# A router stage with its steps pipelined one batch deeper

## The reference

```
h = h + gated @ Wproj + bproj              # gated: the gated heads, (tokens, 256)
x = layernorm(h)                           # over the 256 columns of a token
logits = x @ router_w.T + experts_bias     # (tokens, 8)
rw, sel = top_k(logits, 2); rw = softmax(rw)
moe = sum over the 2 chosen experts of rw * (silu(x w1) * (x w3)) w2,  plus a shared expert
```

## Time and profile before

| | us |
|---|---|
| median of 3 runs | 1509.64 |
| profiled execution, first to last instruction | 1589.0 |
| block `out_route` in it, about | 845 to 955 |
| PE, DVE, ACT busy in 843 to 957 | 71.1, 58.0, 41.8 of 114 |
| granted TensorE clock in 843 to 957 | 0.75 |

### The profile page before, as it was taken

One profiled execution on the slowest core, in us unless ns is written; L12 is line 12 of the kernel. 1 busy time (PEld: TensorE's weight loads), 2 busy tenths in 40 slices (PEclk: granted clock), 3 DMA queues, 4 the chain that ended last, 5 costly groups with the idle time before them and its releaser, 6 DMA issues. The chain is left out here.

```text
span 1589.0 us, 29472 instructions
## 1 busy us (share of the span) xinstructions
PE 1285.5 (81%) x9695; PEld 992.9 (62%) x9696; DVE 852.7 (54%) x1794; ACT 662.1 (42%) x1260; POOL 664.7 (42%) x616
## 2 busy tenths in 40 slices
PE   6878999999978769918996767129986999989997
PEld 3655555555557657706664547119985888878886
DVE  4996677676738849965553554104432333333332
ACT  3872556555655544403453332003332333333332
POOL 7856566665341206772000001760002454544553
PEclk9995799888989977858997778558997999999999
DMA  1678889888300036643533110000017534365331
GB/s 50 195 254 247 231 241 250 232 233 212 89 1 1 1 106 185 184 130 88 119 68 115 44 40 8 8 1 27 33 34 267 129 53 125 59 196 130 54 53 21
DMA packets 122865, 179.26 MB, mean 113 GB/s; under 512 B 26052, under 2 KB 83820, under 8 KB 122772
## 3 DMA queue, kind: packets, MB, share of 16 engines
q1 hardware_dynamic: 105876, 159.62, 34.5%
q0 software_dynamic: 16896, 18.44, 6.9%
HBM read 104.73 MB, written 74.31 MB: 113 GB/s over the span
## 5 line engine op out<-in xcount | busy, mean ns | idle before, releaser
L1629 DVE TENSOR_REDUCE att_top<-att_psS 128x4 f32<-128x512 f32 (+2 forms) x192 | 195.2, 1039 | 79.4 <-PE att_psS L1516 78.8
L2773 POOL DMA_INDIRECT out<-ffn1c_y,ffn1c_table x72 | 113.3, 1574 | 179.4 <-ACT ffn1c_y L2886 91.0
L2762 POOL DMA_INDIRECT ffn1c_rows<-normed_rows,ffn1c_table x72 | 71.0, 987 | 151.1 <-DVE ffn1c_gate L2934 127.4
L2914 DVE TENSOR_TENSOR ffn1c_hid<-ffn1c_psG,ffn1c_sil 128x512 f32<-128x512 f32 x72 | 49.8, 692 | 144.9 <-PE ffn1c_psG L2814 144.9
L1600 ACT ACTIVATE att_prob<-att_psS 128x1024 f32<-128x1024 f32 (+1 forms) x96 | 83.7, 886 | 78.7 <-PE att_psS L1530 78.6
L1510 PE MATMUL att_psS<-pairs_ka,pairs_qa 48*128 48x384 f32 (+3 forms) x512 | 107.4, 428 | 8.3 <-DMA pairs_ka<-k_parts 4.1
L2814 PE MATMUL ffn1c_psG<-ffn1c_w_h,ffn1c_xh 128*128 x288 | 97.5, 420 | 11.5 <-DMA ffn1c_w_l<-experts_lo 4.7
L1600 ACT ACTIVATE pairs_part<-att_psS 128x1024 f32<-128x1024 f32 (+1 forms) x96 | 83.3, 887 | 52.1 <-PE att_psS L1530 52.1
L1530 PE MATMUL att_psS<-pairs_qa,pairs_ka 50*128 50x256 f32 (+3 forms) x512 | 95.7, 418 | 3.3 <-DVE att_top L1629 1.1
L2650 DVE TENSOR_TENSOR ffn1b_act_f<-ffn1b_psG,ffn1b_sil 128x256 f32<-128x256 f32 x64 | 27.2, 425 | 126.4 <-remote 63.3
L2814 PE MATMUL ffn1c_psG<-ffn1c_w_l,ffn1c_xh 128*128 x288 | 91.0, 397 | 0.0
(11 more groups left out here) (397 smaller groups left out, 3577.4 us busy)
## 6 DMA issues: line engine op xcount, KB each, us to landing
prep_raw<-in_w_all SPq DMA_DIRECT2D x27, 512.0 KB, 6.9
experts_hi<-ffn0w_room SPq DMA_DIRECT2D x27, 512.0 KB, 3.9
experts_lo<-prep_lo SPq DMA_DIRECT2D x27, 512.0 KB, 4.7
ffn1c_w_h<-experts_hi SPq DMA_DIRECT2D x8, 1536.0 KB, 6.5
ffn1c_w_l<-experts_lo SPq DMA_DIRECT2D x8, 1536.0 KB, 10.9
qkv_near<-near_keys SPq DMA_DIRECT2D x32, 320.0 KB, 4.3
q_parts<-pairs_part SPq DMA_DIRECT2D x8, 1024.0 KB
k_parts<-pairs_part SPq DMA_DIRECT2D x16, 512.0 KB
```

The lines of the kernel that those rows point to most:

```text
L1629: dve.tensor_reduce(dst, src, AX.X, ALU.max).then_inc(s["max"], 1)
L2762: pool.indirect_dma_start(out=rows[:, t.buf, :], out_offset=None, in_=dram["rows"], in_offset=bass.IndirectOffsetOnAxis(ap=table[:, t.valu ...
L2773: pool.indirect_dma_start(out=rows_out, in_=y[:, t.buf, :], in_offset=None, out_offset=bass.IndirectOffsetOnAxis(ap=table[:, t.value:t.val ...
L2914: dve.tensor_tensor(hid[:, t.par, :], psG[:, t.par, 1, :], sil[:, t.par, :], ALU.mult).then_inc(s["act"], 1)
```

## The change

The steps are reordered and one more is added (B+3). In step n, PE now projects batch n, turns the logits of n-3, turns rows of n-1, turns attention of n+2 and makes logits of n-2. Two batches of attention are turned and split on PE and ACT before the loop. ACT's list becomes: copy the sums of n-3, split rows of n-1, split attention of n+2, root of n, normed n. DVE adds each half of the projection and at once takes its statistics, then aggregates; it splits rows before it adds the bias; bias and pick are of n-3. The turned sums get a bank of their own, `psL`, with the waits that go with it. DVE's wait for the bias load comes after the first `low_attention`.

```diff
--- before.py
+++ after.py
@@ -116,8 +116,14 @@
             k.sem(f"{name}_{n}") for n in "stats mv dev root rstd shift".split())
 
     def dve_gather(self, dve, res, b):
-        for t in range(TG * b, TG * (b + 1)):
+        self.dve_stats(dve, res, range(TG * b, TG * (b + 1)))
+        self.dve_aggregate(dve, b)
+
+    def dve_stats(self, dve, res, tiles):
+        for t in tiles:
             dve.bn_stats(self.stats[:, t, :], res[:, t, :]).then_inc(self.s_stats, 1)
+
+    def dve_aggregate(self, dve, b):
         for t in range(TG * b, TG * (b + 1)):
             dve.wait_ge(self.s_stats, t + 1)
             dve.bn_aggr(self.mv[:, t, :], self.stats[:, t, :]).then_inc(self.s_mv, 1)
@@ -2135,7 +2141,7 @@
         none = k.sb("none", [P, D])
         empty = k.sb("empty", [P, TILES, 2], I32)
         psA, psX = k.ps("psA", [P, KD, S]), k.ps("psX", [P, KD, S])
-        psY, psR = k.ps("psY", [P, 2, 512]), k.ps("psR", [P, 512])
+        psY, psR, psL = k.ps("psY", [P, 2, 512]), k.ps("psR", [P, 512]), k.ps("psL", [P, 512])
         s = {n: k.sem(n) for n in ("bias hi wt names logT0 none empty filler blank aT ah al y res xn xT xh xl logT_ps logT "
                                    "log_ps log best place placef gap exp hot share").split()}
         s_raw = [k.sem(f"raw{n}") for n in range(len(ws))]
@@ -2214,7 +2220,7 @@
             def logits(b):
                 pe.wait_ge(s["xl"], KD * (b + 1))
                 if b >= 1:
-                    pe.wait_ge(s["log"], b)
+                    pe.wait_ge(s["logT"], b)
                 n = 0
                 for m, x in split_passes(w_r["hi"], w_r["lo"], xh, xl):
                     for c in range(KD):
@@ -2224,23 +2230,26 @@
 
             def turn_logits(b):
                 pe.wait_ge(s["logT"], b + 1)
+                if b >= 1:
+                    pe.wait_ge(s["log"], b)
                 for i in range(TG):
-                    mm = pe.transpose(psR[:, P * i:P * (i + 1)], logT[:, P * i:P * (i + 1)], ident[:])
+                    mm = pe.transpose(psL[:, P * i:P * (i + 1)], logT[:, P * i:P * (i + 1)], ident[:])
                 mm.then_inc(s["log_ps"], 1)
 
             turn_attention(0)
+            turn_attention(1)
             pe.wait_ge(s["wt"], len(ws))
-            for n in range(B + 2):
+            for n in range(B + 3):
+                if n < B:
+                    project(n)
+                if 0 <= n - 3 < B:
+                    turn_logits(n - 3)
+                if 0 <= n - 1 < B:
+                    turn_rows(n - 1)
+                if n + 2 < B:
+                    turn_attention(n + 2)
                 if 0 <= n - 2 < B:
                     logits(n - 2)
-                if n + 1 < B:
-                    turn_attention(n + 1)
-                if n < B:
-                    project(n)
-                if 0 <= n - 2 < B:
-                    turn_logits(n - 2)
-                if 0 <= n - 1 < B:
-                    turn_rows(n - 1)
 
         @block.scalar
         def _(act):
@@ -2268,19 +2277,21 @@
             def logits(b):
                 act.wait_ge(s["logT0"], 1)
                 act.wait_ge(s["logT_ps"], b + 1)
+                if b >= 1:
+                    act.wait_ge(s["log_ps"], b)
                 act.copy(logT[0:E1N, :], psR[0:E1N, :]).then_inc(s["logT"], 1)
 
             high_attention(0)
-            for n in range(B + 2):
-                if 0 <= n - 2 < B:
-                    logits(n - 2)
-                if n + 1 < B:
-                    high_attention(n + 1)
+            high_attention(1)
+            for n in range(B + 3):
+                if 0 <= n - 3 < B:
+                    logits(n - 3)
+                if 0 <= n - 1 < B:
+                    high_rows(n - 1)
+                if n + 2 < B:
+                    high_attention(n + 2)
                 if n < B:
                     own.act_root(act, tiles_of(n), n)
-                if 0 <= n - 1 < B:
-                    high_rows(n - 1)
-                if n < B:
                     normed(n)
             act.wait_ge(s["gap"], 1)
             act.activation(gap[:], gap[:], ACT.Exp).then_inc(s["exp"], 1)
@@ -2295,11 +2306,10 @@
                     dve.tensor_tensor(al[:, b % 2, c, :], psA[:, c, :], ah[:, b % 2, c, :].bitcast(F32), ALU.subtract
                                       ).then_inc(s["al"], 1)
 
-            def add(b):
-                for q in range(2):
-                    dve.wait_ge(s["y"], 2 * b + q + 1)
-                    r = res[:, TG * b + 2 * q:TG * b + 2 * q + 2, :]
-                    dve.tensor_tensor(r, r, psY[:, q, :].rearrange("p (t d) -> p t d", d=D), ALU.add).then_inc(s["res"], 1)
+            def add(b, q):
+                dve.wait_ge(s["y"], 2 * b + q + 1)
+                r = res[:, TG * b + 2 * q:TG * b + 2 * q + 2, :]
+                dve.tensor_tensor(r, r, psY[:, q, :].rearrange("p (t d) -> p t d", d=D), ALU.add).then_inc(s["res"], 1)
 
             def low_rows(b):
                 for c in range(KD):
@@ -2309,7 +2319,7 @@
 
             def logits(b):
                 dve.wait_ge(s["log_ps"], b + 1)
-                dve.tensor_tensor(log[:, tiles_of(b), :], psR[:].rearrange("p (t c) -> p t c", c=P)[:, :, 0:E1N],
+                dve.tensor_tensor(log[:, tiles_of(b), :], psL[:].rearrange("p (t c) -> p t c", c=P)[:, :, 0:E1N],
                                   bias[:].unsqueeze(1).to_broadcast([P, TG, E1N]), ALU.add).then_inc(s["log"], 1)
 
             def pick(b):
@@ -2320,24 +2330,26 @@
                     dve.wait_ge(s["best"], t + 1)
                     dve.max_index(place[:, t, :], best[:, t, :], log[:, t, :]).then_inc(s["place"], 1)
 
+            low_attention(0)
             dve.wait_ge(s["bias"], 16)
-            low_attention(0)
-            for n in range(B + 2):
+            for n in range(B + 3):
                 if n + 1 < B:
                     low_attention(n + 1)
                 if n < B:
-                    add(n)
-                    dve.wait_ge(s["res"], 2 * n + 2)
-                    own.dve_gather(dve, res, n)
+                    for q in range(2):
+                        add(n, q)
+                        dve.wait_ge(s["res"], 2 * n + q + 1)
+                        own.dve_stats(dve, res, range(TG * n + 2 * q, TG * n + 2 * q + 2))
+                    own.dve_aggregate(dve, n)
                     own.dve_dev(dve, tiles_of(n), n)
-                if 0 <= n - 2 < B:
-                    logits(n - 2)
                 if 0 <= n - 1 < B:
                     low_rows(n - 1)
+                if 0 <= n - 3 < B:
+                    logits(n - 3)
                 if n < B:
                     own.dve_scale(dve, tiles_of(n), n)
-                if 0 <= n - 2 < B:
-                    pick(n - 2)
+                if 0 <= n - 3 < B:
+                    pick(n - 3)
             dve.wait_ge(s["best"], NT)
             dve.tensor_tensor(gap[:], best[:, :, 1], best[:, :, 0], ALU.subtract).then_inc(s["gap"], 1)
             dve.wait_ge(s["place"], NT)
```

## The result

The kernel after takes 1469.51 us (median of 4 runs, 1459.12 to 1475.09), the kernel before 1508.31 us (4 runs). The ratio is 0.9752, 95% interval 0.971 to 0.9794: 31 to 44 us faster. The forecast of 1480.4 lies 10.9 us too high. Medians and ratios in this document leave out one run of `ends` (1554.07 us) that fell in a slower state.

The account below looks back on a forecast made before the run. Waits in one circle, not a full engine, bound the block; the last normed 33.6 us earlier less 2.1 of tail gave 31.5, scaled to 29.9, less 0.7 is 29.2, so 1480.4 us; range 1470 to 1497.

Parts of the forecast that it names:

- One circle bounds the step: Block before: logits, turned attention, split, add, statistics, root, split rows, logits run almost without overlap, 11.8 us a step.
- A full step of 7.15 us: Middle steps after the change: the longest of three engine lists, 7.1 us, and a little for their meeting.
- lists of 7.1 (rows), 7.0 (DVE) and 6.8 (PE): Full step: time of the chain through rows, of DVE's own work and of PE's own work at 2.4 GHz.
- the rows' circle: Chain from one normed to the next through copy, turned logits and rows, splits, root and scale: 7.1 us with hand-offs.
- a meeting of the lists: Full step: a little added to the longest list of 7.1 us, giving 7.15.
- PE stays at the high level in the middle: Middle of the block: granted clock above 0.9, PE's work priced at 2.4 GHz, 6.8 us a step.
- The rival of a falling clock: PE's clock falls in each step, 7 steps lose 2.0 us each, total 1493 us; chance 0.15.
- The bank costs no time: Turned sums' own bank: case without it bounded by 0 and one DVE wait of 0.65 us, taken as 0.
- The bias wait frees turned attention: Block's head: moved bias load frees batch 1's turned attention earlier; first normed still ends at 862.5 (-1.2 to +1.5).
- The tail grows by 2.1 us: From the last normed to gap: 12.6 us priced at 1.2 GHz, against 10.5 before.
- Scaling the gain by 0.950: Whole kernel: timed runs are 0.950 of the profiled span, so the 31.5 us gain was scaled to 29.9.
- The give-back of 0.7 for unseen waits: Whole kernel: 0.7 us taken off the scaled gain of 29.9 us, leaving 29.2.

Follow-up runs that it names:

- ends: Kernel after, with the square-root table loaded at the block's start and the tail reordered: 1540.95 us, ratio to before 0.9709.
- att_shallow: Kernel after, with attention turned for batch n+1 instead of n+2, all else kept: ratio to before 1.0039, block 112.96 us.
- deep_alone: Kernel before, with attention turned for batch n+2 instead of n+1 and nothing else changed: ratio to before 1.0017, block 107.7 us.
- pick_last2: Kernel after, with all picks of DVE moved behind the loop: one execution, steps of 6.76 us, block 75.93 us.
- before_again: Kernel before, unchanged, run for a second profile: span 1575.2 us, block 103.95 us.

## Why the prediction was right, and where it was off

- *One circle bounds the step.* Right. `att_shallow` puts turned attention back into the circle and the whole gain is gone; `deep_alone` shows that depth without the new order doesn't cut it.
- *A full step of 7.15 us, from lists of 7.1 (rows), 7.0 (DVE) and 6.8 (PE).* The step is 6.82. I had the rows' circle as the longest list; it is DVE's, by 0.06 us. DVE has no wait in the steps of 6.82, and in `pick_last2`, where it has waits, the circle runs at 6.76. PE's list is 6.6 (6.82 less the wait of 0.20). The three terms were each 0.2 to 0.35 too high: I summed durations where the rows of successive operations overlap by 0.1 to 0.25 on ACT and PE (turned attention 881.85, logits 882.64: 0.79 apart, its row says 1.04), and added 0.05 for a meeting of the lists that didn't cost anything.
- *PE stays at the high level in the middle.* 1.00 in each stretch of the middle, 0.93 over the block. The rival of a falling clock did not come up in after; it does in `att_shallow`, and the wait before it is 3.6 us there, 0.2 here. One reading behind it was too strong: not every logits row of before is at the lower level. The first row at 940.53 takes 0.64 after a wait of 3.42 us, and `before_again` has two such.
- *The bank costs no time, bounds 0 and 0.65, taken 0.* As a price of the case without the bank, this was wrong. Without it a full step is 0.95 us longer, above my bound, and the block 10.7. I looked for its worth in the waits of before, where the turned sums had a whole phase of the step, and not in the new order, where logits follow them at once. The forecast of the total didn't suffer, since the change has the bank.
- *The bias wait frees turned attention, but the first `normed` stays.* It came 2.3 us earlier; the mis-sized term. My bound reached 1.2.
- *The tail grows by 2.1 us.* It shrank by 0.3 against the profile that I had. I priced it at 1.2 GHz, but most of it runs at 2.4: only the last rows and the logits of batch 6 fell (1.64 and 1.20). The old tail varies as well: in `before_again`, with its last logits at the high level, it is 8.7 us, and against that the tail did grow, by 1.6.
- *Scaling the gain by 0.950.* That was a wrong reading of the 79 us between the profile and the median. They lie in one stretch of another block (71.8 us), not spread over the kernel, so the block's gain holds in full. Unscaled, my sum of 31.5 gives 1478.1 from the first median; the block's measured 37.5 gives 1472.1, and the measured median of after is 1469.5. The give-back of 0.7 for unseen waits wasn't needed either.

The sum was thus 6.0 us short in the block: 2.3 in the head, 1.3 in the steps, 2.4 in the tail. With 1.6 for the scaling and 0.7 for the give-back this makes 8.3 of the 10.9 us; the other 2.6 are within the runs' spread. These terms all missed the same way, so none hid another.

## What to carry to other kernels

Where three engines hand one batch around in a circle, look for depth and order together: here each was worth nothing alone. The producer was moved a step ahead, and the work that had waited longest was put at the end of the list. Price a new bank or buffer in the new order; the waits of the old one don't show its worth. Before scaling a gain by profiled over timed time, find the stretch in which the two differ; and read such a change by the length of its block, which for the kernel after repeated within 0.1 us while its whole times spread by 16.

## What the runs showed of the hardware

- The same kernel has two lengths, by the chip or set of runs: 1582 and 1509 us for before. Of the 76.5 us between the spans of the two profiles of after (1473.4 and 1549.9), 72.0 lie in one stretch of 1154 matmuls (167.0 and 238.9). Its cause is open.
- Filler matmuls of 24 x 0.13 us in an idle stretch of TensorE made the whole kernel 0.8% faster (ratio 0.9918, 0.988 to 0.9955): the logits behind them ran at the high level, 0.63 us a row instead of 1.02.
- ScalarE's table load for the square root takes 1.28 us. Moved from behind the third split to the start of the block, it shortened the head from 15.16 to 13.91 us.
